# Attention scores issued two units at a time, and a reordered passage from set-up to main loop

## What is computed

```
q = split_heads(x @ w_q)
out_text = sdpa(q, split_heads(text @ w_k), split_heads(text @ w_v))
out_ip   = sdpa(q, split_heads(ip @ w_k_ip), split_heads(ip @ w_v_ip), mask=mask_ip)
out = (out_text + out_ip) @ w_out + b_out + x
```

## Time and profile before

| | us |
|---|---|
| runs, median (lowest to highest) | 820.23 (819.54 to 821.26) |
| the profiled execution's own time | 820.14 |
| its span, first to last instruction | 818.3 |
| PE, DVE, POOL, ACT busy | 795.8, 676.2, 627.7, 541.3 |
| mean granted TensorE clock | 0.989 |

### The profile page before, as it was taken

The page is one execution under the profiler, slowest core; times in us unless marked ns, Lnnn a source line. Parts: engine busy times, 40 slices in busy tenths (PEclk is TensorE's granted clock), DMA queues, the critical chain, the costliest instruction groups (busy, mean ns, idle before and its releaser), DMA issues.

```text
span 818.3 us, 12921 instructions
## 1 busy us (share of the span) xinstructions
PE 795.8 (97%) x4381; PEld 648.8 (79%) x4381; DVE 676.2 (83%) x983; ACT 541.3 (66%) x928; POOL 627.7 (77%) x576
## 2 busy tenths in 40 slices
PE   9999889999999999999999999999999999999687
PEld 8889767888888878888787888878787887887466
DVE  6838767889878897889878888889888987888973
ACT  7766376677586667666785767676676757675632
POOL 0049648797987888797979888787979898788962
PEclk9999989999999999999999999999999999999999
DMA  9933587564767577764766487766766476465654
GB/s 314 391 125 113 175 271 235 179 230 141 240 213 220 189 231 219 231 213 140 265 182 212 160 255 220 223 201 183 253 192 243 130 240 211 155 194 180 194 185 162
DMA packets 104177, 169.99 MB, mean 208 GB/s; under 512 B 13104, under 2 KB 56112, under 8 KB 103984
## 3 DMA queue, kind: packets, MB, share of 16 engines
q1 hardware_dynamic: 103968, 167.86, 63.9%
q10 hardware_dynamic: 144, 1.31, 0.4%
HBM read 103.26 MB, written 65.54 MB: 206 GB/s over the span
## 4 chain that ended last, share of the span: by engine, by line
PE 88%; POOL 3%; DVE 3%; ACT 2%; SPq 1%; DMA 1%; issue 1%; DVEq 0%; ACTq 0%
PE bank L101 23%; PE bank L102 21%; PE bank L103 21%; PE bank L197 10%; PE bank L1176 4%; PE bank L1177 4%; PE bank L1061 1%; PE bank L1069 1%; PE bank L1073 1%; POOL prob L246 1%; POOL oT_lo L579 1%; DMA xin<-in_xT 1%; POOL pT_lo L583 1%; DVE wo_lo L846 1%; POOL prob L253 1%
## 5 line engine op out<-in xcount | busy, mean ns | idle before, releaser
L735 ACT ACTIVATE pv_part<-bank 64x512 f32<-64x512 f32 x160 | 94.7, 592 | 173.5 <-PE bank L1177 171.1
L246 POOL TENSOR_TENSOR prob<-prob,top 128x896 f32<-128x896 f32 (+1 forms) x160 | 184.0, 1170 | 14.8 <-DVE top L217 14.7
L253 POOL TENSOR_TENSOR prob<-prob,inv 128x896 f32<-128x896 f32 (+1 forms) x160 | 170.3, 1086 | 11.6 <-DVE inv L225 10.4
L101 PE MATMUL bank<-oT_hi,wo_hi 128*128 128x512 f32 x400 | 165.9, 415 | 3.6 <-POOL oT_lo L579 3.6
L966 DVE TENSOR_TENSOR o_raw<-bank,pv_part 64x512 f32<-64x512 f32 x160 | 110.1, 688 | 63.0 <-ACT pv_part L735 59.7
L101 PE MATMUL bank<-xT_hi,wq_hi 128*128 128x512 f32 x400 | 156.6, 392 | 2.6 <-DVE v_ip L938 2.6
L102 PE MATMUL bank<-oT_lo,wo_hi 128*128 128x512 f32 x400 | 157.7, 394 | 0.0
L103 PE MATMUL bank<-oT_hi,wo_lo 128*128 128x512 f32 x400 | 157.6, 394 | 0.0
L102 PE MATMUL bank<-xT_lo,wq_hi 128*128 128x512 f32 x400 | 156.1, 390 | 0.0
L103 PE MATMUL bank<-xT_hi,wq_lo 128*128 128x512 f32 x400 | 156.1, 390 | 0.0
L579 POOL TENSOR_TENSOR oT_lo<-o_raw,oT_hi 128x512 fp32r<-128x512 f32 x80 | 110.5, 1381 | 54.2 <-ACT oT_hi L739 52.5
(11 more groups left out here) (103 smaller groups left out, 1229.5 us busy)
## 6 DMA issues: line engine op xcount, KB each, us to landing
p_scratch<-stage SPq DMA_DIRECT2D x80, 512.0 KB, 3.0
prob<-p_scratch SPq DMA_DIRECT2D x320, 128.0 KB, 3.1
res<-in_xT SPq DMA_DIRECT2D x80, 256.0 KB, 4.7
outT<-res SPq DMA_DIRECT2D x80, 256.0 KB, 3.9
xin<-in_xT SPq DMA_DIRECT2D x75, 256.0 KB, 4.8
w_raw<-in_L_xattn_w_k SPq DMA_DIRECT2D x8, 320.0 KB, 5.6
w_raw<-in_L_xattn_w_k_ip SPq DMA_DIRECT2D x8, 320.0 KB, 6.2
w_raw<-in_L_xattn_w_v_ip SPq DMA_DIRECT2D x8, 320.0 KB, 4.3
```

Of the source, the lines that this page charges most:

```text
L101: nc.tensor.matmul(dst, a_hi, b_hi, start=first, stop=False)
L246: ins = nc.gpsimd.tensor_tensor(s, s, top[:, m, n, :].unsqueeze(2).broadcast_to([P, ROWS, k1 - k0]), ALU.subtract)
L253: ins = nc.gpsimd.tensor_tensor(s, s, inv[:, m, n, :].unsqueeze(2).broadcast_to([P, ROWS, k1 - k0]), ALU.mult)
```

## The change

1. **Couples.** Units 1 and 3 write the values banks (`v_bank`), units 0, 2 and 4 `l_bank`. Units 1 and 2 are issued together in slot 1, units 3 and 4 in slot 3, each time after the output steps and the first 9 of 15 matmuls of the slot's query product; the other 6 follow. The waits that the shared banks need come with it: units 1 and 3 for `add_pv` of the slot's pairs, pairs 4, 5, 8 and 9 for the copies out of `v_bank`, and `copy_scores` of units 2 and 4 for the `pT_part` of the old chunk.
2. **Orders.** ACT, DVE and POOL get new orders: `exponentials(n, 4)`, `sums(n, 4)` come before the group ends instead of after; `normalise(g, 3)` and `turn(g, 3)` after its start instead of before; `maxima(n, 0)`, `turn(g, 4)`, `x_lo_part(x, 4)` and DVE's `pT_part(g, 4)` ahead of `output(g-1, 0)`. SP hands over chunks 3 and 4 together, ahead of the stores, and chunks 0, 1 and 2 one by one.
3. **Passage.** Group 1's last query product moves from ahead of the loop into slot 0 of group 0, behind unit 0, into `o_bank[2]`; ACT's and DVE's order of group 0 is changed for it. DVE's two `v_ip` additions move ahead of a weight chunk and two turns.

```diff
...
         return l_bank[(m + 1) % 2]
     if g == 1 and m < 3:
         return l_bank[(m + 1) % 2]
+    if g == 1 and m == KD - 1:
+        return o_bank[2]
     return e_bank if m < KD - 1 else l_bank[0]
 def q_steps(pe, g, m, k0=0, k1=KD):
...
     sp.dma_start(k_raw[:].rearrange("p m k -> p (m k)"), k_scratch[:, b, :]).then_inc(k_raw_loaded, 16)
 def s_bank(g, n):
-    return bank[n % 6] if g == 0 else l_bank[n % 2]
+    if g == 0:
+        return bank[n % 6]
+    return (v_bank if n // 2 in (1, 3) else l_bank)[n % 2]
 v_raw_loaded, v_zeroed, v_hi_built, v_built = (sem(n) for n in ("v_raw_loaded", "v_zeroed", "v_hi_built", "v_built"))
...
                 ins.then_inc(score_ready, 1)
 def copy_scores(act, g, m):
+    if g > 0 and m in (2, 4):
+        act.wait_ge(pT_lo_dve, KD * (g - 1) + m + 1)
+        act.wait_ge(pT_lo_pool, KD * (g - 1) + m + 1)
     for n in (2 * m, 2 * m + 1):
         act.wait_ge(score_ready, UNITS * g + n + 1)
         nc.scalar.activation(score_dst(n), s_bank(g, n)[:].rearrange("p (t c) -> p t c", c=PW), ACT.Copy).then_inc(score_copied, 1)
...
             b = g // GPB
             if g + 3 < NG:
                 load_x(g + 3)
+            hand_over(g, (3, 4) if g > 0 else (4,))
             if g > 0:
                 for m in OUT_ORDER:
                     store(g - 1, m)
-            hand_over(g, (4,))
             for m in OUT_ORDER:
                 load_res(g, m)
             if g % GPB == 0 and b < B - 1:
...
                 load_k(sp, b + 1)
                 load_v(b + 1)
             if g + 1 < NG:
-                hand_over(g + 1, (0, 1))
-                hand_over(g + 1, (2, 3))
+                for m in range(3):
+                    hand_over(g + 1, (m,))
         for m in OUT_ORDER:
...
         for g in range(NG):
             n = g + 1
             more = n < NG
+            if g > 0:
+                normalise(pool, g, 3)
+            if more:
+                add_mask(pool, n, 0)
             oT_part(g, 0)
-            if more:
-                add_mask(pool, n, 0)
             if g > 0:
                 normalise(pool, g, 4)
             if more:
                 sub_max(pool, n, 0)
             pT_part(g, 5)
+            oT_part(g, 1)
+            if more:
+                normalise(pool, n, 0)
+            pT_part(g, 7)
             if more:
                 add_mask(pool, n, 1)
-            pT_part(g, 7)
-            oT_part(g, 1)
-            if more:
+                add_mask(pool, n, 2)
                 sub_max(pool, n, 1)
-                normalise(pool, n, 0)
-                add_mask(pool, n, 2)
             oT_part(g, 2)
             if more:
+                sub_max(pool, n, 2)
                 normalise(pool, n, 1)
-                sub_max(pool, n, 2)
+            oT_part(g, 3)
+            pT_part(g, 9)
+            if more:
+                normalise(pool, n, 2)
                 add_mask(pool, n, 3)
-            pT_part(g, 9)
-            oT_part(g, 3)
-            if more:
+                add_mask(pool, n, 4)
                 sub_max(pool, n, 3)
-                normalise(pool, n, 2)
-                add_mask(pool, n, 4)
-                normalise(pool, n, 3)
+            oT_part(g, 4)
+            if more:
                 pT_part(n, 1)
-            oT_part(g, 4)
-            if more:
                 sub_max(pool, n, 4)
                 pT_part(n, 3)
...
             n, x = g + 1, g + 2
             more, more_x = n < NG, x < NG
-            if more:
+            if g == 0:
+                move_pv(g, 0)
+                move_pv(g, 1)
+                copy_scores(act, n, 0)
+                oT_part(g, 0)
                 move_q(act, n, 4)
-            if more_x:
-                split_x(x, 0)
-            move_pv(g, 0)
-            if more_x:
-                split_x(x, 1)
-            move_pv(g, 1)
-            if more_x:
-                split_x(x, 2)
-            if more:
-                copy_scores(act, n, 0)
-            if more_x:
-                split_x(x, 3)
-            if g > 0:
-                exponentials(act, g, 4)
-            if more_x:
-                split_x(x, 4)
-            oT_part(g, 0)
-
-            move_pv(g, 2)
+                for k in range(KD):
+                    split_x(x, k)
+            else:
+                if more:
+                    move_q(act, n, 4)
+                if more_x:
+                    split_x(x, 0)
+                move_pv(g, 0)
+                if more_x:
+                    split_x(x, 1)
+                move_pv(g, 1)
+                if more_x:
+                    split_x(x, 2)
+                if more:
+                    copy_scores(act, n, 0)
+                if more_x:
+                    split_x(x, 3)
+                oT_part(g, 0)
+                if more_x:
+                    split_x(x, 4)
             pT_part(g, 4)
             pT_part(g, 5)
+            if more:
+                exponentials(act, n, 0)
+
+            move_pv(g, 2)
             move_pv(g, 3)
             pT_part(g, 6)
+            oT_part(g, 1)
+            pT_part(g, 7)
             if more:
                 copy_scores(act, n, 1)
-            pT_part(g, 7)
-            oT_part(g, 1)
-            if more:
-                exponentials(act, n, 0)
-
-            move_pv(g, 4)
+                copy_scores(act, n, 2)
+
             if more_x:
                 move_q(act, x, 0)
-            if more:
-                copy_scores(act, n, 2)
+            move_pv(g, 4)
             move_pv(g, 5)
+            oT_part(g, 2)
             if more:
                 exponentials(act, n, 1)
-            oT_part(g, 2)
-
-            move_pv(g, 6)
+
             if more_x:
                 move_q(act, x, 1)
-            if more:
-                copy_scores(act, n, 3)
+            move_pv(g, 6)
             move_pv(g, 7)
             pT_part(g, 8)
             pT_part(g, 9)
+            oT_part(g, 3)
             if more:
                 exponentials(act, n, 2)
-            oT_part(g, 3)
-
-            move_pv(g, 8)
+                copy_scores(act, n, 3)
+                copy_scores(act, n, 4)
+
             if more_x:
                 move_q(act, x, 2)
+            move_pv(g, 8)
             move_pv(g, 9)
             if more and n % GPB == 0:
                 v_hi_part(n // GPB)
-            if more:
-                exponentials(act, n, 3)
-                copy_scores(act, n, 4)
             oT_part(g, 4)
             if more_x and x % GPB == 0:
                 act.wait_ge(score_ready, UNITS * x)
...
             if more:
                 pT_part(n, 0)
                 pT_part(n, 1)
+                exponentials(act, n, 3)
                 pT_part(n, 2)
             if more_x:
                 move_q(act, x, 3)
             if more:
+                exponentials(act, n, 4)
                 pT_part(n, 3)
     @block.vector
...
             lo_chunk(c)
         x_lo_part(dve, 1, 4)
         out_chunks = [c for c in mine if c >= WO0]
+        for n, (i, c0, c1) in enumerate(V_IP_BANKS):
+            dve.wait_ge(v_ip_moved, n + 1)
+            nc.vector.tensor_tensor(v_ip[:, c0:c1], bank[i][0:TI, 0:c1 - c0], v_ip_lo[:, c0:c1], ALU.add).then_inc(v_ip_added, 1)
         lo_chunk(out_chunks[0])
         turn(dve, 0, 0)
         turn(dve, 0, 1)
-        for n, (i, c0, c1) in enumerate(V_IP_BANKS):
-            dve.wait_ge(v_ip_moved, n + 1)
-            nc.vector.tensor_tensor(v_ip[:, c0:c1], bank[i][0:TI, 0:c1 - c0], v_ip_lo[:, c0:c1], ALU.add).then_inc(v_ip_added, 1)
         for i in range(BLOCKS - 1):
             if i == 1:
                 lo_chunk(out_chunks[1])
...
             n, x = g + 1, g + 2
             more, more_x = n < NG, x < NG
-            if more_x:
+            if more_x and g > 0:
                 x_lo_part(dve, x, 0)
             add_pv(g, 0)
             add_pv(g, 1)
+            if g == 0:
+                maxima(dve, n, 0)
+                x_lo_part(dve, x, 0)
             if more_x:
                 x_lo_part(dve, x, 1)
                 x_lo_part(dve, x, 2)
             if g > 0:
+                turn(dve, g, 3)
                 output(g - 1, 3)
             if more_x:
                 x_lo_part(dve, x, 3)
+            if more and g > 0:
+                maxima(dve, n, 0)
+            turn(dve, g, 4)
+            if more_x:
+                x_lo_part(dve, x, 4)
             if g > 0:
-                sums(dve, g, 4)
                 output(g - 1, 4)
+            pT_part(g, 4)
+            if g > 0:
                 output(g - 1, 0)
-            if more:
-                maxima(dve, n, 0)
-            if g > 0:
                 output(g - 1, 1)
                 output(g - 1, 2)
-            if more_x:
-                x_lo_part(dve, x, 4)
             add_pv(g, 2)
-            pT_part(g, 4)
             add_pv(g, 3)
-            turn(dve, g, 4)
-            if more:
+            if more:
+                sums(dve, n, 0)
+            pT_part(g, 6)
+            if more:
+                turn(dve, n, 0)
```

(45 more changed lines are left out.)

4 lines of the change are left out of this document (2 added, 2 removed).

## The result

| | before | after |
|---|---|---|
| runs, median (lowest to highest), us | 819.88 (817.85 to 821.26) | 900.20 (894.20 to 901.54) |
| ratio, 95% interval | | 1.097 [1.094, 1.100] |
| profiled execution: own time, span | 820.14, 818.3 | 901.54, 899.7 |
| mean granted TensorE clock | 0.989 | 0.954 |

The change makes the kernel 9.7% slower. The forecast was 868 with a range of 828 to 892. The direction and the two places of the waits were right; the size was too small, and 900.2 lies outside the range.

What follows compares the result with a forecast made beforehand. PE was taken as the bound (97% busy, no wait in a whole group). Waits of 34.0 us in odd and 24.3 in even groups, less 10.4 for couples, gave +47.9 on 820.14: 868 us, range 828 to 892.

Steps and rivals of the forecast that it cites:

- the two places of the waits: PE would wait at unit 0 for `move_q(n, 4)` and at slot 1's first output steps for `output(g-1, 0)`.
- couples: Two score units in a row on PE save 0.40 us a couple, 10.4 us in groups 1 to 13.
- odd groups, waits: Seven odd groups wait 1.75 us at unit 0 and 3.1 at slot 1: 34.0 us.
- even groups, waits: Six even groups wait 0.2 us at unit 0 and 3.85 at slot 1: 24.3 us.
- passage; groups 14 and 15: Passage into the loop through group 0, and the last two groups: 0 each, bounds -4 to +4 each.
- a rival with 0.24: Waits over 3 us drop TensorE from 2.4 to 1.2 GHz, 1.7 us lost 13 times: 890 us; chance 0.24.
- The wait at unit 0: PE at unit 0 in odd groups, for ACT's late `move_q`: 1.3 to 1.8 us, taken as 1.75.
- the exclusion: DVE's differences ahead of `output(g-1, 0)` cannot overlap POOL's work: 2.1 us (odd), 2.5 (even), bounds 0 and 4.
- `x_lo` 3 behind `normalise`: DVE's `x_lo` 3 held behind POOL's `normalise` 4: up to 1.3 us, taken as 0.6.
- `x_lo` 0: DVE's `x_lo` 0 held behind POOL's `normalise` 3: 0.5 us in odd groups, 0.9 in even ones.
- the alternation of groups: Full groups would show alternating lengths near 48 to 49 us.
- the mechanism at slot 1: Longer DVE chain, PE 1.29 us earlier and overlaps with POOL make PE wait 3.1 (odd) or 3.85 us (even).

Runs made afterwards that it cites:

- experiment 1: Kernel after, with unread matmuls filling PE's waits: 15 before slot 1's first output step, 6 before unit 0 in odd groups; 880.58 us, ratio 1.074.
- experiment 9: Kernel of experiment 8 plus 15 unread matmuls ahead of slot 1's first output step in groups 1 to 13; 866.36 us, ratio 1.057.
- experiment 4: Kernel after, with DVE's two-operand differences replaced by one-operand reductions of like length, leaving out DVE's lo parts; 835.10 us, ratio 1.019.
- experiment 11: Kernel before with couples and reordered engines, plus POOL's `pT_part(n, 1)` before `normalise(n, 3)` and DVE's `x_lo_part(x, 3)` behind `output(g-1, 0)`; 823.35 us, ratio 1.0046.
- experiment 8: Kernel after, with POOL's `sub_max(n, 4)` moved ahead of `pT_part(n, 1)`; 898.47 us, ratio 1.097.
- experiment 2: Kernel after, with DVE's `output(g-1, 4)` and `(g-1, 0)` to `(g-1, 2)` ahead of `turn(g, 4)`, `x_lo_part(x, 4)` and `pT_part(g, 4)`; 891.48 us, ratio 1.088.

## Why the prediction was wrong

The profiled execution, against the forecast's terms for groups 1 to 13. The low clock is what those 13 groups take (662.9 us) beyond seven of 50.0 and six of 48.4, the lengths that a group has without it (group 6 for the even ones, experiment 1 for both). Against the 13 groups of experiment 1 themselves it is 21.2.

| term | forecast | measured |
|---|---|---|
| couples | -10.4 | -10.4 (2 x 0.40 x 13; the traces give 0.39 and 0.41) |
| odd groups, waits | 7 x 4.85 = 34.0 | 7 x (50.0 - 44.33) = 39.7 |
| even groups, waits | 6 x 4.05 = 24.3 | 6 x (48.4 - 44.33) = 24.4 |
| low clock | 0 | 22.5 |
| passage; groups 14 and 15 | 0; 0 | +2.7; +2.5 |
| sum | +47.9 | +81.4 |

- **The step that failed: the clock was left out of the sum.** I had the waits (over 3 us each, in 13 groups) and the two rows in which such a gap was followed by a granted clock of 0.66, priced them at 22 us, and put that beside the forecast as a rival with 0.24. It was a consequence of the forecast's own waits, not another way for things to go. The measured term is 22.5. That the two figures agree so well is partly luck: I had one stretch a group, and two groups had none, others held twice as much. With it the sum is 890, still inside the range; what takes the profiled execution to 901.5 are the next two points, the passage and the last groups. Experiments 1 and 9 show the clock's part from the other side. No case of the prediction reached 900.
- **Waits in odd groups, 0.8 us each too small.** The wait at unit 0 was 1.8 as taken. At slot 1 I had 3.1 and PE waited 3.76: the exclusion costs 3.1 us there (experiment 4), not 2.1. In DVE's timeline the six differences ahead of the output cost, beyond 0.68 each, 0.1, 0.2, 0, 1.5, 0.6 and 0.8 us (odd groups, in the chain's order). The mis-sized term is the fourth, `x_lo` 3 behind `normalise`, which I took as 0.6; `x_lo` 0, taken as 0.5 and 0.9, cost 0.1 and 0. In even groups the sum of the two was right to 0.02; that is partly luck, for the exclusion cost 3.0 and not 2.5 there, and the rest of the chain was 0.6 shorter than I had it.
- **Right:** the price of a couple, both places, the alternation of groups, the mechanism at slot 1 (chain longer, PE earlier, exclusion). That a group comes out shorter by what the couples save, once the waits are taken off, is seen most plainly in experiment 11.
- **Passage.** Unit 1 could not start before about 121.9, I wrote; it started at 123.5, behind a wait of 3.29 us, and its 32 records took 3.78 us at the low clock. Of the PE timeline in group 0:

```profile
123.53 3.78 PE L201 MATMUL bank<-k_diag,qT 64*128 64x128 f32 x32 [3.29 <-DVE o_raw L979]
```

Group 1 starts at 154.4, 2.7 late, and most of that is the clock again: in experiment 8, where group 0 has the same wait of 3.29 us, it starts at 149.8 (group 0 takes 43.9 us at a granted clock of 0.96 and not 47.6 at 0.87). The reordered passage itself is within the +-4 that I gave it. I did not run it without the rest of the change.

## What to carry to other kernels

When a forecast puts a regular wait of some microseconds on TensorE, what this trace shows behind such waits belongs in the same sum; it is no rival. Here eleven groups of 13 had low stretches, 1.7 us a group on the average of the 13. An order in which one engine's two-operand work is moved must be read against what the other engine does in that very moment: with one difference moved to where POOL's own differences stand, the kernel took 11 us more. And ahead of giving PE less to do, ask what each other chain needs of a group: here the 0.8 us saved on PE could not be had in any order tried; the shortest groups with couples were 45.07 and 45.55 us, where all had been 45.13.

## What the runs showed of the hardware

- A DVE difference of two operands (128x512) that starts while a POOL operation is running ends 0.545 to 0.555 us behind the end of that operation: in 69 of 92 cases in the kernel before and in 104 of 106 after. Of the other cases before, 14 ended ahead of POOL's operation, mostly 0.67 us long as if alone; in 13 of them it was POOL's difference that took long, 2.13 us where it takes 1.29. Six more started within 0.05 us of POOL's end and took their usual 0.69. The Trainium skill, SBUF — State Buffer, section on the two separate sides, has the exclusive lock; that DVE's work nearly whole (0.55 of 0.68) follows POOL's end is what the rows add. The reductions of one operand in experiment 4 were not touched.
- The clock does not answer to one wait alone. In the kernel after, a wait of 3.59 us by the profile's count was followed by a low stretch in most groups, but not in groups 6 and 12; in group 5 the 1.79 at unit 0 was followed by one (0.83 and 0.60 granted over 363 to 366 and 366 to 369), and the 1.98 at slot 1 by another. In experiment 2, with waits up to 2.3, the mean clock stayed at 0.984 in one execution and was 0.971 to 0.977 in three. What decides between these I leave open.
